# Transposed x of chunks 1 to 3 by DMA transposes of f16 row splits, three weight buffers, another ScalarE order in chunk 0, and the square root as a power on GpSimd

## What is computed

```python
xn = (x - mean(x)) / sqrt(var(x) + 1e-5)
q, k, v = (einsum('bpd,hde->bphe', xn, W) + b for W, b in ...)
scores = where(causal, einsum('bqhe,bkhe->bhqk', q, k) / sqrt(128), -1e5)
s = einsum('bqhe,hed->bqd', einsum('bkhe,bhqk->bqhe', v, softmax(scores)), W_O) + b_O
hdn = silu(xn @ gate_w.T * gate_s) * (xn @ up_w.T * up_s)      # 1408 hidden units
g = silu(hdn @ down_w.T * down_s)
return x + s * g
```

## Time and profile before

| | us |
|---|---|
| three runs | 1154.16, 1153.47, 1157.09 |
| median | 1154.16 |
| span of the profiled execution | 1154.1 |
| chunk 0: first gate matmul to the first of chunk 1 | 13.88 to 84.84 |
| chunks 1 to 3 | 84.84 to about 265 |
| attention | about 265 to 1154.1 |

### The profile page before, as it was taken

One profiled execution on the slowest core, in us unless ns is written; L12 is line 12 of the kernel. 1 busy time (PEld: TensorE's weight loads), 2 busy tenths in 40 slices (PEclk: granted clock), 3 DMA queues, 4 the chain that ended last, 5 costly groups with the idle time before them and its releaser, 6 DMA issues.

```text
span 1154.1 us, 23252 instructions
## 1 busy us (share of the span) xinstructions
PE 1125.5 (98%) x5772; PEld 547.8 (47%) x5772; DVE 729.6 (63%) x1587; ACT 575.7 (50%) x1276; POOL 84.1 (7%) x104
## 2 busy tenths in 40 slices
PE   5999999999999999999999999999999999999987
PEld 3344444444444544544444545444445454554443
DVE  6665364435776666666666666666666666677775
ACT  5754353334565544555455545555555444455532
POOL 1000000003000000000000000000000000134373
PEclk9999999999999999999999999999999999999989
DMA  6401111112444334333444334333444633346545
GB/s 227 167 30 43 45 56 55 55 48 64 97 92 89 82 77 82 82 77 77 85 89 87 77 77 86 77 77 80 88 90 80 114 60 59 86 114 187 118 118 132
DMA packets 236756, 101.77 MB, mean 88 GB/s; under 512 B 219456, under 2 KB 219456, under 8 KB 236736
## 3 DMA queue, kind: packets, MB, share of 16 engines
q1 hardware_dynamic: 231200, 85.78, 33.9%
q0 software_dynamic: 3424, 11.54, 3.3%
q10 hardware_dynamic: 2112, 4.19, 1.0%
HBM read 38.57 MB, written 8.39 MB: 41 GB/s over the span
## 4 chain that ended last, share of the span: by engine, by line
PE 88%; DVE 3%; DMA 3%; ACT 3%; issue 2%; SPq 0%; ACTq 0%; DVEq 0%
PE bank L436 79%; PE bank L589 8%; DMA arena<-arena 2%; PE bank L449 1%; ACT arena L824 1%; ACT arena L837 1%; DMA arena<-ffn_w_dram 1%; DVE row_max L1062 1%; DVE arena L1080 0%; SPq L335 0%; DMA arena<-x_dram 0%; DVE bank L1056 0%; DVE arena L888 0%; ACT V_hi L817 0%; DVE arena L1147 0%
## 5 line engine op out<-in xcount | busy, mean ns | idle before, releaser
L436 PE MATMUL bank<-XT_hi,arena 128*128 (+1 forms) x1392 | 453.3, 380 | 2.8 <-issue 2.7
L436 PE MATMUL bank<-XT_lo,arena 128*128 (+1 forms) x864 | 328.0, 380 | 0.0
L436 PE MATMUL bank<-arena 128*128 (+1 forms) x1124 | 268.3, 380 | 1.2 <-DVE arena L1087 1.0
L824 ACT ACTIVATE arena<-bank,neg_max 128x512 f32<-128x512 f32 (+3 forms) x256 | 132.6, 524 | 216.2 <-DVE neg_max L1066 216.1
L436 PEld LDWEIGHTS bank<-XT_hi,arena 128*128 (+1 forms) x1392 | 136.4, 98 | 161.9 <-issue 7.0
L436 PEld LDWEIGHTS bank<-arena 128*128 (+1 forms) x1124 | 107.6, 98 | 126.2 <-issue 13.4
L436 PE MATMUL bank<-arena,XT_hi 128*128 (+1 forms) x512 | 152.3, 379 | 0.0
L1080 DVE SCALAR_TENSOR_TENSOR arena<-arena,inv_sum 128x512 f16<-128x512 f32 (+3 forms) x256 | 144.2, 625 | 4.3 <-ACT arena L837 4.3
L436 PEld LDWEIGHTS bank<-XT_lo,arena 128*128 (+1 forms) x864 | 84.7, 98 | 92.7 <-issue 0.8
L837 ACT ACTIVATE arena<-arena,inv_sum 128x512 f16<-128x512 f32 (+3 forms) x256 | 122.3, 558 | 0.8 <-DVE inv_sum L1072 0.8
L589 PE MATMUL bank<-arena,V_hi 128*128 128x512 f16 x504 | 111.0, 301 | 3.3 <-DMA arena<-arena 3.0
(11 more groups left out here) (83 smaller groups left out, 1085.8 us busy)
## 6 DMA issues: line engine op xcount, KB each, us to landing
w_in<-attn_w_dram SPq DMA_DIRECT2D x64, 256.0 KB, 2.6
arena<-ffn_w_dram SPq DMA_DIRECT2D x11, 768.0 KB, 5.3
arena<-x_dram SPq DMA_DIRECT2D x16, 256.0 KB, 4.0
parked_silu<-arena ACTq DMA_DIRECT2D x4, 1024.0 KB, 4.5
arena<-x_dram POOLq DMA_DIRECT2D x12, 256.0 KB, 2.9
arena<-parked_silu POOLq DMA_DIRECT2D x12, 256.0 KB, 3.0
out_dram<-arena POOLq DMA_DIRECT2D x12, 256.0 KB, 2.8
arena<-arena SPq DMA_TRANSPOSE x128, 4.2
```

The lines of the kernel that those rows point to most:

```text
L436: mm = nc.tensor.matmul(out, stationary(a, k), moving(b, k), start=first and n == 0 and i == 0, stop=last and n == len(tiles) - 1 and i == ...
L824: e = nc.scalar.activation(probs[:, at:at + width], SC[b_][:, col:col + width], ACT.Exp, bias=neg_max[:, i:i + 1], scale=SCORE_SCALE, accu ...
```

## The change

1. **x of chunks 1 to 3 is turned by DMA.** ScalarE and VectorE split the scaled x row by row (token on the partition) into `XS` (`split_rows`), which lies where `V` will lie in attention. SP then issues a DMA transpose for each of the four row tiles and each half, straight into `XT` (`turn_rows`): 8 per chunk, 24 in all. TensorE transposes only chunk 0, and waits for `xt_turned` ahead of a chunk. SP's load of the next chunk's x follows the transposes of a chunk; for chunk 3 the transposes stand between loads of attention weights.
2. **Three weight buffers** `FFN_IN` (`FB = 3`); the third lies in the same tensor as `V`. SP loads three tiles at the start and refills a buffer three tiles later.
3. **ScalarE in chunk 0**: the tables are gone. Ahead of step 0 it splits tiles 0 to 2; in step m, between the silu and the copy of `hidden`, it splits tile m+3 and sums tile m+2 (`first_chunk`, `amid`); in steps 7 and 8 it also splits two row tiles of x each. VectorE splits tile m+3 behind step m, and its statistics, scaling and row splits are spread over steps 2 to 8.
4. **Square root**: for chunks 1 to 3 GpSimd computes `var_eps ** -0.5` (`ALU.pow` on 128x4 numbers), and the reciprocal on VectorE falls away. Chunk 0 keeps its square root on ScalarE.

The core of the diff:

```diff
@@ sync
+            def load_ffn(m):
+                if m >= FB:
+                    sp.wait_ge(fw_lo, 3 * (m - FB + 1))
+                sp.dma_start(FFN_IN[m % FB], ffn_w[m]).then_inc(ffn_loaded[m % FB], 16)
...
+            for m in range(5, MT):
+                load_ffn(m)
+            def turn_rows(c, tiles=range(TT)):
+                for t in tiles:
+                    for part, split in ((0, xs_hi), (1, xs_lo)):
+                        sp.wait_ge(split, TT * (c - 1) + t + 1)
+                        sp.dma_start_transpose(out=XT[part][:, :, c * S + t * P:c * S + (t + 1) * P],
+                                               in_=XS[part][:, t]).then_inc(xt_turned, 16)
+            for c in range(1, B - 1):
+                turn_rows(c)
+                load_x(c + 1)
...
+                if 4 <= sl < 4 + TT:
+                    turn_rows(B - 1, (sl - 4,))
@@ gpsimd
+            for c in range(1, B):
+                pool.wait_ge(var_ok, c + 1)
+                nc.gpsimd.tensor_tensor(rstd0[:], var_eps[:], minus_half[:], ALU.pow).then_inc(std_ok, 1)
@@ tensor
-                    pe.wait_ge(xt_lo, KT * (c + 1))
+                    pe.wait_ge(xt_turned, 16 * 2 * TT * c)
...
-                    for k in range(2):
-                        transpose_x(c + 1, k)
-                    steps(c, 6, 10, exact)
-                    for k in range(2, KT):
-                        transpose_x(c + 1, k)
@@ scalar
+            def split_rows(c, tiles):
+                if c > 1 and tiles[0] == 0:
+                    act.wait_ge(xt_turned, 16 * 2 * TT * (c - 1))
+                for t in tiles:
+                    act.wait_ge(xn_ok, TT * c + t + 1)
+                    nc.scalar.activation(XS[0][:, t], x_in[:, t], ACT.Copy).then_inc(xs_hi, 1)
...
+            split_ffn(1)
+            split_ffn(2)
             act.wait_ge(const_scaled, 3)
+            step(0, 0, 0, amid=lambda: sum_lo(0))
+            split_ffn(3)
+            sum_lo(2)
+            def first_chunk(m):
+                if m + 3 < MT:
+                    split_ffn(m + 3)
+                if m + 2 < MT:
+                    sum_lo(m + 2)
+                if m in (7, 8):
+                    split_rows(1, (0, 1) if m == 7 else (2, 3))
+            for m in range(1, MT - 1):
+                step(0, m, m % 2, amid=lambda: first_chunk(m))
@@ vector
+                if m == 0:
+                    max_lo(DVE_LO)
+                if m + 3 < MT:
+                    split_ffn(m + 3)
+                if 2 <= m < 2 + TT:
+                    token_stats(1, (m - 2,))
+                if m == 5:
+                    variances(1)
+                if m in (6, 7):
+                    scale_x(1, (0, 1) if m == 6 else (2, 3))
+                if m in (7, 8):
+                    split_rows(1, (0, 1) if m == 7 else (2, 3))
```

More of the change, by code:

```diff
@@ L151, in build @@
         XT = [sb(f"XT_{n}", [P, KT, T], F16) for n in ("hi", "lo")]
-        V = [sb(f"V_{n}", [P, 2, TT, HG * E], F16) for n in ("hi", "lo")]
+        v_hi_lo = sb("V", [P, 2 * 2 * TT * HG * E], F16)
+        V = [v_hi_lo[:].rearrange("p (s b t n) -> p s b t n", s=2, b=2, t=TT)[:, part] for part in (0, 1)]
+        XS = [v_hi_lo[:, part * TT * D:(part + 1) * TT * D].rearrange("p (t d) -> p t d", t=TT) for part in (0, 1)]
+        third = v_hi_lo[:, 2 * TT * D:2 * TT * D + 2 * 3 * 512].bitcast(F32)
+        FFN_IN = [part.rearrange("p (w n) -> p w n", w=3) for part in (ffn_in[:, :3 * 512], ffn_in[:, 3 * 512:], third)]
         Q = [sb(f"Q_{n}", [P, S], F16) for n in ("hi", "lo")]
@@ L211, in build @@
         xt_lo = sem("xt_lo")
-        ffn_loaded = [sem("ffn_loaded0"), sem("ffn_loaded1")]
+        xs_hi = sem("xs_hi")
+        xs_lo = sem("xs_lo")
+        xt_turned = sem("xt_turned")
+        ffn_loaded = [sem(f"ffn_loaded{i}") for i in range(FB)]
         fw_hi = sem("fw_hi")
@@ L795, in _ @@
                 if c < B - 1:
-                    step_and_slice(c, 2, 0)
-                    root(c + 1)
-                    step_and_slice(c, 3, 1)
-                    steps(c, 4, 6)
-                    split_x(c + 1, 0)
-                    split_x(c + 1, 1)
+                    steps(c, 2, 4)
+                    step_and_slice(c, 4, 0)
+                    split_rows(c + 1, (0, 1))
+                    step_and_slice(c, 5, 1)
+                    split_rows(c + 1, (2, 3))
                     steps(c, 6, 10)
@@ L975, in end_chunk @@
             def end_chunk(c):
[L976 to L979 removed]
+                step(c, MT - 1, 2)
                 step(c + 1, 0, 0, down_of=c)
```

172 lines of the change are left out of this document (64 added, 108 removed).

## The result

The changed kernel takes 1146.74 us (median of four executions, 1146.24 to 1147.36); the kernel before took 1155.59 beside it. The ratio is 0.9924, 95% interval 0.9909 to 0.9939. A second measurement on another chip gave 1148.52 against 1155.41 (0.9934, 0.9917 to 0.9951). The forecast was 1146.2, with a range of 1143.0 to 1150.5.

The account below looks back on a forecast made before the run. TensorE was taken as the bound, busy 1125.5 of 1154.1 us. Transposes -5.2, square root -0.3 and chunk 0 -2.4 sum to -7.9, giving 1146.2 us, range 1143.0 to 1150.5.

Parts of the forecast that it names:

- The sum: Whole kernel: -5.2 - 0.3 - 2.4 = -7.9 us, giving 1146.2 us.
- two groups: Chunk 0: two groups of eight TensorE transposes leave the path, 0.87 us each.
- four groups: Chunks 1 and 2, turning x for chunks 2 and 3: four groups of eight TensorE transposes go, 0.87 us each.
- TensorE transposes, -5.2: FFN chunks: 48 transposes leave TensorE, six groups at 0.87 us each on the path, -5.2 us.
- The hand-carried chain: Chunk 0 followed gate by gate: step 3 at 33.8, step 7 at 56.4, gate 9 at 70.1, gate 10 at 75.5.
- DMA transposes: SP turning x: 1 us issue and 3 us landing each; chunk 1's last lands near 77, hidden.
- The rival on the slow side: DMA transposes for chunk 1 run one at a time; 4.2 us each gives 1163, a loss from 3.0 each; chance 0.03.
- another rival: TensorE's clock falls again behind the 1.8 us hole ahead of gate 9, costing 1.7 us: 1147.9; chance 0.18.
- Power on GpSimd, -0.3: Chunk 2: square root leaves ScalarE, interval 5.48 becomes 5.18, -0.3 us; GpSimd's power takes 0.5 us, hidden.
- Chunk 0, -2.4: Third buffer and ScalarE's new order: first-check hole of 2.39 us goes, some given back ahead of gate 9, -2.4 us.
- the 1.7: Behind the first check of chunk 0: 3.4 us at the lower clock level, half of which, 1.7 us, is lost.

Follow-up runs that it names:

- the other base: Changed kernel with ScalarE's row copies of x in steps 7 and 8 behind the copy of the hidden tile: 1146.39 us, FFN interval 231.32.
- the root behind step 6: Changed kernel with square roots of chunks 1 to 3 back on ScalarE, chunk 1's behind step 6 of chunk 0: 1148.89 us, ratio 0.9951.
- two buffers: Changed kernel with two weight buffers, the old order of weight work, and ScalarE's row copies behind the hidden copy: 1149.24 us, ratio 0.9951.
- power alone: Kernel before with only the square roots of chunks 1 to 3 made a power on GpSimd: 1154.00 us, ratio 0.9996.
- transposes one at a time: Changed kernel with SP waiting for each DMA transpose of x to land before issuing the next: 1153.33 us, ratio 0.9988.
- A root placed one step too early: Changed kernel with square roots of chunks 1 to 3 back on ScalarE, chunk 1's behind step 5 of chunk 0: 1151.48 us, ratio 0.9968.

## Why the prediction was right

**The sum.** -7.9 was forecast, and the FFN interval fell by 8.03 us. That it is so close is in part luck, since two misses cancel. From the first hidden tile to that of step 0 of chunk 1 the forecast was -4.1 (two groups and the -2.4), and -4.58 was measured; behind it the forecast was -3.8 (four groups and the -0.3), and -3.45 was measured, since the new interval of 5.54 took 0.36. Nor do the parts add up one by one: taken out singly, TensorE's groups are worth 3.1, the buffers with the order 2.5 (3.3 by the other base) and the power 1.2, 6.8 to 7.6 in all.

**TensorE transposes, -5.2.** Right in the unit: the six intervals of 6.17 and 5.96 are gone, and the groups measured 0.87 when they were put back. But the price of the substitute stood in another part of my sum, so the two parts taken apart mislead: on the chip the DMA way is worth 3.1, since in chunk 0 its row splits cost what two groups had cost. The hand-carried chain had this (2.4 given back, "late, since ScalarE also has two row copies"), and the sum held for that reason.

**DMA transposes.** Mis-sized both ways: SP takes 1.26 us each where I took 1, a landing 2.5 where I took 3. The last landed at 77.4, "near 77", since the two errors cancel in part: seven issues took longer, and the last landing was shorter. The Trainium skill (Advanced Engine Details and Errata, X-Bar Transpose (TRN2)) has them as fast as regular DMAs. The issues of after agree in part: a transpose of 128 KB (128x512 in f16, SBUF to SBUF) takes the same time as a plain load of 256 KB. How much of either is a fixed part, no run shows.

```profile
w_in<-attn_w_dram SPq DMA_DIRECT2D x64, 256.0 KB, 2.6
...
XT_hi<-V SPq DMA_TRANSPOSE x12, 2.5
```

**The rival on the slow side** was right as a mechanism and wrong in its price: I had the loss begin at 3.0 us each, by counting TensorE's wait alone. At 2.45 each the wait itself came out as the rule gives it (7 x 2.45 from 67.9 on ends at 85.1, and TensorE started at 85.11), but the measured loss was 7.4 of a gain of 8.0. The hole brings a fall of the clock, which I had priced, in another rival, at 1.7 and which cost 3.2 here. So, by an estimate from these figures, the loss begins near 2.5 us each.

**Power on GpSimd, -0.3.** The step that failed, though it moved the sum little. The 5.48 became 5.18 as said; the power took 1.01 to 1.05 us where I took 0.5, hidden; the new 5.54 cost what was won. What I missed is worth: I priced the edit on the kernel before. On the changed one it is worth 1.2 us (against the root behind step 6), without which the rest would have brought 6.8 in place of 8.0.

**Chunk 0, -2.4.** Every gate within 0.7 us of the forecast. The hole ahead of gate 9 was 1.60 for 1.8 and made of the very instructions named. The buffers and the order were not tried apart, so which of them closes the hole at the first check is argued from the chain, not shown. Missed: the constants that the third weight tile pushes back by 1.6 us and more. "Third weight buffer ... from the start" adds 768 KB ahead of them on SP, and I looked only at who waits for the tile.

**The clock.** It did not fall at 1.60 us. But the length of a hole doesn't tell it alone: it fell behind 1.89 us (two buffers) and not behind 2.24 us (power alone, at the same check), and behind 4.22 us it stayed low twice as long as behind 2.39. A chance, as I gave it, was the right form. What a fall costs depends on what comes behind it. The kernel with the power alone has the chunk 0 of before and no fall at the first check:

```profile
28.49 0.19 PE L550 MATMUL bank<-lo_sums,ones 128*1 128x3 f32 x2 [2.24 <-ACT lo_abs L720]
...
38.09 0.39 PE L442 MATMUL bank<-XT_hi,arena 128*128 128x512 f16 x1 [1.91 <-issue]
```

Its gate of step 3 comes 9.60 us after the check; before, with the fall, it comes 9.87 us after it, since the hole ahead of the gate was 1.19 us there in place of 1.91. So the fall of the earlier trace rows cost at most 0.3 us before, and not the 1.7 that the prediction reads from the window: gate 3 waited for its flag either way. The sum does not rest on the 1.7; the price of the rival does.

**Against the median.** I made no correction between span and time. The profiled execution of after has 1.5 us outside the span (1.3 in the executions of before whose span is on record), so the forecast of 1146.2 stands against a span of 1144.7. The 1.1 us in attention, 0.24 us by which the first hidden tile came sooner, and 0.1 of the sum brought the span down by what the time has on top: that 1146.24 matches 1146.2 is luck. Median against median the change is worth 8.9 us, and the medians of before beside the experiments lie between 1154.35 and 1155.74, all above the 1154.16 that I started from.

## What to carry to other kernels

Price each part on the kernel that the whole change makes: the same edit was worth 0 before and 1.2 us after, and a substitute's work on the engines that set the flag cost two fifths of what the replaced work gave back. When a load is put earlier, look at what comes behind it in the same queue, not only at who waits for it. For effects below the spread of the times, compare an interval inside the trace that repeats within 0.1 us, and check on a second execution that it does. And the price of a fall of the clock is read from the next gate behind it, not from the window alone.

## What the runs showed that I had not expected

- An instruction added to VectorE, with no reader, made a kernel faster by 0.38 us (FFN interval 230.29 to 229.91).
- A root placed one step too early cost over three times what it costs in its place (4.16 and 1.21 us). With it came one wait of 2.35 us on ScalarE and a fall of TensorE's clock; the two were not taken apart.
- Two executions of the same kernel differ by 2.8 us in their last 45 us, by the landing of one DMA transpose (6.73 and 9.22 us) and by whether the clock falls behind it.
- A fall of the clock for 3.4 us cost at most 0.3 us in one place (the first check of before) and one for 6.8 us cost 3.2 us in another (transposes one at a time).
